# A four-layer network on one core: the start and a norm of the last layer joined with their neighbours, and a 15-tap convolution by even and odd samples

## Time and profile before

| what | value |
|---|---|
| median of three runs | 2219.96 us (2219.67 to 2226.17) |
| the profiled execution, its own time | 2215.92 us |
| its span, first to last instruction | 2214.2 us |
| busy: PE, DVE, ACT, POOL | 83%, 73%, 55%, 30% |
| mean granted TensorE clock | 0.90 of full speed |

### The profile page before, as it was taken

The page is one execution under the profiler, slowest core; times in us unless marked ns, Lnnn a source line. Parts: engine busy times, 40 slices in busy tenths (PEclk is TensorE's granted clock), DMA queues, the critical chain, the costliest instruction groups (busy, mean ns, idle before and its releaser), DMA issues. The chain is left out here.

```text
span 2214.2 us, 45686 instructions
## 1 busy us (share of the span) xinstructions
PE 1846.9 (83%) x17745; PEld 992.8 (45%) x17751; DVE 1612.4 (73%) x2720; ACT 1216.6 (55%) x2472; POOL 674.7 (30%) x755
## 2 busy tenths in 40 slices
PE   2888877866647999999988889999788979887987
PEld 1222221443221335963233357776564434555755
DVE  5999999785779997569963955554756649876367
ACT  2999999532333886258866245556433620221475
POOL 1112120321675542124444633330214620000160
PEclk7899899987876999999989989999789979998986
DMA  8422430100551532733321122212001341430310
GB/s 280 91 58 58 97 77 1 77 19 6 136 190 30 123 59 79 209 76 68 50 32 45 43 65 66 65 53 80 11 23 46 123 142 75 141 94 13 119 53 34
DMA packets 156703, 171.87 MB, mean 78 GB/s; under 512 B 55468, under 2 KB 125174, under 8 KB 156482
## 3 DMA queue, kind: packets, MB, share of 16 engines
q1 hardware_dynamic: 142904, 144.03, 23.8%
q0 software_dynamic: 13584, 24.92, 4.5%
HBM read 95.58 MB, written 77.28 MB: 78 GB/s over the span
## 5 line engine op out<-in xcount | busy, mean ns | idle before, releaser
L464 ACT ACTIVATE a_E<-a_scores,a_nmax 128x512 f32<-128x512 f32 x512 | 343.2, 814 | 14.2 <-DVE a_nmax L397 13.2
L1057 ACT ACTIVATE a_E<-a_scores 128x512 f32<-128x512 f32 x512 | 273.8, 601 | 97.2 <-PE a_scores L1092 92.1
L397 DVE TENSOR_REDUCE a_nmax<-a_scores 128x2 f32<-128x1024 f32 x256 | 302.5, 1217 | 20.8 <-PE a_scores L479 17.1
L961 DVE TENSOR_REDUCE a_nmax<-a_first 128x2 f32<-128x1024 f32 x256 | 295.6, 1217 | 15.2 <-PE a_first L1082 14.0
L479 PE MATMUL a_scores<-a_Vh,a_Kh 48*128 48x512 bf16 x512 | 108.2, 421 | 96.0 <-ACT a_E L464 71.9
L1082 PE MATMUL a_first<-a_Kh,a_Qh 48*128 48x512 bf16 x512 | 148.2, 417 | 36.8 <-PEq L51 20.1
L492 PE MATMUL a_turn<-a_E,a_QS 128*32 128x256 f32 x2048 | 174.1, 417 | 2.3 <-DVE a_QS L407 1.8
L464 ACT ACTIVATION_READ_ACCUMULATOR a_E<-a_scores,a_nmax 128x1 f32 x512 | 167.0, 334 | 0.0
L1092 PE MATMUL a_scores<-a_Qh,a_Kh 51*128 51x512 bf16 x512 | 161.0, 396 | 5.1 <-PEq L51 1.9
L1114 PE MATMUL a_out<-a_E,a_V 128*32 128x256 f32 x2048 | 162.7, 398 | 0.0
L2193 POOL DMA_INDIRECT outs<-f_ye,f_row_at x80 | 78.2, 977 | 144.7 <-ACT f_ye L2314 112.5
(11 more groups left out here) (599 smaller groups left out, 4422.6 us busy)
## 6 DMA issues: line engine op xcount, KB each, us to landing
f_up<-in_L_up SPq DMA_DIRECT2D x32, 256.0 KB, 3.3
a_Kh<-a_rows_k SPq DMA_DIRECT2D x16, 384.0 KB, 6.5
a_Vh<-a_rows_v SPq DMA_DIRECT2D x16, 384.0 KB, 9.9
a_Qh<-a_rows_q SPq DMA_DIRECT2D x32, 192.0 KB, 4.9
a_Kh<-a_rows_k SPq DMA_DIRECT2D x32, 192.0 KB, 5.7
slots<-empty SPq DMA_DIRECT2D x8, 645.0 KB, 6.4
f_xe<-slots SPq DMA_DIRECT2D x40, 129.0 KB, 2.1
outs<-zeros SPq DMA_DIRECT2D x8, 512.0 KB, 4.7
```

Of the source, the lines that this page charges most:

```text
L397: v.tensor_reduce(nmax[:, rd % 2, r1, :, q], bank(b, u)[:], AX.X, ALU.max, negate=True).then_inc(S["max_ready"], 1)
L464: m = a.activation(E[:, u % NE, x], bank(b, u)[:, x], ACT.Exp, bias=nmax[:, rd % 2, r1, x, q:q + 1], accum_out=Z[:, rd % 2, r1, x, q:q + 1])
L961: v.tensor_reduce(out, slot_bank(n)[:], AX.X, ALU.max, negate=True).then_inc(S["slot_read"], 1)
L1057: a.activation(E[:, u % NE, x], ps_s[n % 3][:], ACT.Exp, scale=SCALE).then_inc(S["exp_ready"], 1)
```

## The change

Four edits.

1. **Start.** Blocks one to three become one. x comes in five transfers, the first two of one sequence each; ACT issues the seven weight transfers instead of SP; sequence 0 is normed, turned, projected and split ahead of the others; k is spilled by SP and v by ACT; the first head of each quarter is loaded apart from the others, and the attention's first unit waits for those alone, its ninth for the rest. The parts of sequence 1 are made in block four by POOL. Filling the slots and the small loads move to SP's list in block four, behind the load of each next sequence. ACT splits `parts[2]` instead of POOL, and POOL clears `QS` instead of DVE.
2. **Norm and mix of the last layer.** The three blocks become one: `rows` comes straight from x with a second reciprocal root (variance times (1 + eps), plus eps squared), and turning `rows`, the mix, and turning `XN` go in turns, with one bank each for s, o and the two turned forms.
3. **Inputs of the last attention.** ACT: both sigmoids of q and k, then the gate, then the sigmoid of v. POOL: two row transfers ahead of the gated product instead of one on each side.
4. **Convolution.** For a pair of sequences: y_even from the even taps on even samples (8 products), y_odd from the odd taps on odd samples (7), and one filter of the sums of neighbouring taps on the sums of neighbouring samples (8); each product has 2 x 256 columns. So 92 products instead of 120. POOL adds the taps and the samples and puts the outputs together; ACT copies the banks. The three fetches of expert weights come after all of it, since their room is used for the sums.

```diff
-def attention0(nc, g, w, ahead):
+def load_first_rows(eng, rows, dst, sem, first):
+
+    for x in range(2):
+        src = rows.rearrange("(x q i d) t s -> x (d t) q i s", x=2, q=2, d=HD)[x]
+        heads = dst[64 * x:64 * x + HD * TERMS].rearrange("p (q i) s -> p q i s", q=2)
+        for q in range(2):
+            if first:
+                eng.dma_start(heads[:, q, 0], src[:, q, 0]).then_inc(sem, 16)
+            else:
+                eng.dma_start(heads[:, q, 1:4], src[:, q, 1:4]).then_inc(sem, 16)
...
+                    statistics(0)
+                    variances(0, 0, 1)
+                    roots(0, 0, 1)
+                    normalise(0, R)
...
+                    take_k(v, ps[0][:, 0]).then_inc(S["k_ready"], 1)
+                    v.wait_ge(S["v_made"], 1)
+                    take_v(v, ps[0][:, 1]).then_inc(S["v_ready"], 1)
...
+                    spill_right(a, rows_v[0], parts[:, :, T:2 * T], S["v_spilled"])
+                    query(0)
+                    root(2, EARLY, NB)
+                    a.activation(spare[:], g.ident[:, 0:1], ACT.Exp)
+                    taken(1)
+                    taken(2)
+                    taken(3)
+                    query(1)
+                    for b in range(4, NB):
+                        taken(b)
...
                     load(sp, b, b % 2)
+                    beside(sp, b)
...
-            layer_norm(nc, g, "3", g.X, g.XN, g.XT, ahead=load_weights, again=True)
-            g.recycle_sems()
-            layer_norm(nc, g, "3a", g.XN, rows, HT, scale=ln_cols[:, 0:1], bias=ln_cols[:, 1:2], by_row=True)
...
                     for b in range(NB):
+                        if b + 1 < NB:
+                            turn_rows(b + 1)
                         inputs(b)
+                        turn_x(b)
                         if b:
                             outputs(b - 1)
...
-            conv = [(b, s) for b in range(NB) for s in range(MIXED3)]
-            AHEAD, PER = 78, 3
+            PAIRS = NB // 2
+            SIZES = (EVEN, ODD, EVEN)
+            conv = [(j, n, t) for j in range(PAIRS) for n in range(3) for t in range(SIZES[n])]
+            AHEAD, PER = len(conv) - NHB + 2, 1
...
+                    def add_phases(j):
+                        if j:
+                            pool.wait_ge(S["ms_done"], 3 * j)
+                        x = VT[:, 2 * j:2 * j + 2, PAD3 - 2 * LAG:PAD3 + T].rearrange("c b (k e) -> c b k e", e=2)
+                        pool.tensor_tensor(x_pair, x[:, :, :, 0], x[:, :, :, 1], ALU.add).then_inc(S["x_ready"], 1)
+
+                    def put_together(j):
+                        out = MS[:, 2 * j:2 * j + 2].rearrange("c b (k e) -> c b k e", e=2)
+                        pool.wait_ge(S["ms_read"], 3 * j + 2)
+                        pool.tensor_tensor(out[:, :, :, 0], of_even, of_odd[:, :, 0:HALF], ALU.add)
+                        pool.tensor_tensor(of_even, of_even, of_odd[:, :, 1:1 + HALF], ALU.add)
+                        pool.drain()
+                        pool.wait_ge(S["ms_read"], 3 * j + 3)
+                        pool.tensor_tensor(out[:, :, :, 1], of_both, of_even, ALU.subtract).then_inc(S["ms_ready"], 1)
...
+                        for j, n, t in products:
+                            q = 3 * j + n
+                            if t == 0:
+                                if q >= 2:
+                                    pe.wait_ge(S["ms_read"], q if j + 1 == PAIRS else q - 1)
...
+                            if n < 2:
+                                W, lo = G[:, 2 * t + n], PAD3 + n - 2 * t
+                                x = VT[:, 2 * j:2 * j + 2, lo:lo + T - 1:2]
+                            else:
+                                W = G_pair[:, t] if t < ODD else G[:, 2 * ODD]
+                                x = x_pair[:, :, LAG - t:LAG - t + HALF]
...
-                    convolved(conv[:4 * MIXED3])
+                    BEFORE = 2 * sum(SIZES) + EVEN
+                    a.wait_ge(S["G_ready"], 1)
+                    convolved(conv[:BEFORE])
                     a.wait_ge(S["inverted"], 1)
                     for t in range(NG):
                         a.copy(MT[:, t], M[:, t].rearrange("p c e -> p e c")).then_inc(S["solved"], 1)
-                    convolved(conv[4 * MIXED3:AHEAD])
+                        if t == 0:
+                            convolved(conv[BEFORE:BEFORE + ODD])
+                    convolved(conv[BEFORE + ODD:AHEAD])
                     solved(0)
```

More of the change, by code:

```diff
@@ new lines, in normalise, with remainder @@
+                    def normalise(b, rows):
+                        for r in range(rows):
+                            n, s = divmod(b * R + r, 2)
+                            m = v.tensor_scalar(g.XN[:, b, r], g.X[:, b, r], stats[:, n, s, 1:2], rstd[:, n, s:s + 1],
+                                                ALU.subtract, ALU.mult)
+                        m.then_inc(S["xn_ready"], 1)
+                    def remainder(n, src, part, step, done):
+                        cols = slice(n * T, (n + 1) * T)
+                        v.wait_ge(S[step], n + 1)
+                        v.tensor_tensor(rest[:, cols], src[:, cols], parts[:, part, cols], ALU.subtract).then_inc(S[done], 1)
@@ L313, in _, with root @@
[L313 to L318 removed]
+                    def root(n, lo, hi):
+                        ns = slice(lo * R // 2, hi * R // 2)
+                        a.wait_ge(S["var_ready"], n + 1)
+                        a.activation(std[:, ns], var[:, ns], ACT.Sqrt).then_inc(S["std_ready"], 1)
@@ L3442, in _ @@
                 sigmoid(0, 0)
+                sigmoid(0, 1)
+                gate(0)
                 v_sigmoid(0)
-                sigmoid(0, 1)
-                gate_and_squares(0)
+                squares(0)
                 for b in range(NB):
```

482 lines of the change are left out of this document (307 added, 175 removed).

## The result

The changed kernel has a median of 2211.86 us in 20 runs (2189.87 to 2230.5), the kernel before one of 2223.78 in 20 runs beside it (2214.75 to 2236.91). The ratio is 0.9934, with an interval of 0.9912 to 0.9955: 0.7% or 15 us faster. This ratio goes without five slow runs of the changed kernel, those more than 1.5% above its fastest; the medians of all twenty runs of each are 12 us apart. I had forecast 36 us and a range that ended at 2197. The direction was right, the size was not.

A forecast was written before the change was run, and what follows sets the result against it. It took the start as a chain, PE as the mix's bound, DVE as the loop's, with waits for PE. Terms -19.5 - 9.5 - 1 - 6 = -36 turned 2215.9 into 2180, given as 2181 us; range 2168 to 2197.

The forecast's parts named there:

- Edit 1, -19.5: Start: first scores at 31 us instead of 50.6; bounds -25.5 and -13.
- first product to DVE at 10.8: Start, sequence 0: PE's first projection product reaches DVE at 10.8 us, then k's parts are ready at 15.7.
- Edit 2, -9.5: Norm and mix of the last layer: 47.5 us instead of 57, PE-bound at 4.5 a sequence; bounds -13 and -3.
- Edit 3, -1: Inputs of the last attention: the new order on ACT saves 1 us; bounds -3 and +2.
- Edit 4, -6: Convolution: 12 us gained in the loop, 6 us paid for POOL's adds beside DVE.
- (a): Inversion, late taps and loop: 15 POOL adds slow DVE by 0.4 us each, 6 in all; bounds 0 and 13.
- Gain -12: Loop: fewer products make PE's pass about 3.8 us, under DVE's 5.14, so most of DVE's 15.9 us of waits go.
- The term for `mix_taps`: Loop: after a `mix_taps` PE must wait for DVE and runs late, three places, some 4 us in all.
- The wait (b) of my cost side: Ahead of the loop: the last pair's filter waits for ACT's ninth copy until about 1910, just hidden behind DVE; 4 us above.
- The strided read: Convolution: products on every other sample cost PE nothing extra; the nearest earlier rows showed 12% more for weight loads.
- Rival 1: Convolution gives nothing: waits on DVE's path cost 4 us and POOL's adds 10, total 2189; chance 0.18.
- Rival 5: Start not shortened: first loads wait on full DMA queues or ACT or PE is late, 8 us, total 2189; chance 0.09.

The follow-up runs named there:

- start_own_waits: Changed kernel with the first projection waiting for the k and v weights alone, not all seven weight transfers; first scores at 32.2 us instead of 35.7.
- start_clock: Changed kernel with separate weight waits plus unread products of zeros in PE's idle times of the start; first scores at 30.9 us, ratios 0.9869 and 0.9928 to before.
- small_sums: Changed kernel with POOL's output sums and sample sum cut to 4 columns per pair; inversion 55.6 us instead of 61.5, ratio 0.9899 to before.
- no_conv_warm: Changed kernel with the old convolution and 12 unread products ahead of the router; the router began at the upper clock, which fell at about 478 us.

## Why the prediction was wrong

**What bounds.** The stages were chosen rightly. That DVE owns the time from 1827 to the loop stands: edit 4's cost was paid there, in DVE's time. In the loop PE was late before and is late still, which is where edit 4's gain went.

**Edit 1, -19.5: -15.0.** The step that failed is "first product to DVE at 10.8". It came at 14.5, since PE waited for all seven transfers (12.34), and I had put only their issue into the sum, not the landing of the last beside 2 MB of x. k's parts were ready at 19.8, not 15.7. From there on I had 15.3 to the first scores and it took 15.9. start_own_waits takes the wait away and gets 3.5, start_clock gets the forecast 31. Lesson in the same step: I had taken durations of a PE at its upper clock for a PE that had done nothing yet.

**Edit 2, -9.5: -10.** Right, by its own steps: PE stayed the bound, the period is 4.35 for 4.5.

**Edit 3, -1: 0 to +1.** Within its bounds, and within the scatter. The 24.4 us of ACT's wait for POOL went, and ACT waits 44.4 for PE, up from 15.0: idle time of an engine that was not the bound.

**Edit 4, -6: +5.** Two terms failed, the sign with them. (a) "0.4 us each, 6 in all". The mechanism was the named one, its size 9.8 (6.5 in the inversion, 3.3 in the late taps, which I had at 3.2 and 1.2) before the loop's share, which no run separates. I had priced a POOL add by the *median* of the earlier trace rows, 0.97, and these eight rows mix steps under a POOL add with steps beside none; the worst of them, 1.58, was the one that began just behind a POOL add (1745.60 and 1745.54). An add of 1.2 to 2.1 us costs DVE 0.8. The bound of 13 held. (b) "Gain -12": the loops give 4.8 on average, and DVE's wait for PE fell from 18.5 to 12.8 us on average, not to 4. "PE's pass is about 3.8, under DVE's 5.14" counts busy time. PE's work did shrink as I had it, but with one product a pass PE stands still for 17.2 us of the loop on average instead of 7.1 (the 2.19 us in the middle of a solve is one of these times), and its granted clock is lower. I had written "I take no more off for the clock". Why PE stands still stays open. The term for `mix_taps` was right: three waits of PE, 5.9 us in all against "some 4". The wait (b) of my cost side, "just hides behind DVE", came so: both sides are ready within 0.1 us of each other, and without the adds (small_sums) the wait costs 2.3. The strided read costs 5%, between the nil that I took and the 12% of the earlier trace rows, and changes nothing. The Trainium skill ("SBUF — State Buffer", SBUF: two separate sides) calls such a step free; here it is free to within that 5%. The 1.7 to 2.5 ns an element that the Trainium skill ("Vector Engine (DVE) Microarchitecture Reference", Measured stream behaviour on trn2) has for DVE, where adjacent words take 1.05, does not carry over to PE.

**What was in no term.** -15 - 10 + 0.5 + 5 is -19.5; measured are -15 by the ratio and -12 by the medians. The router with the early start took 9 us more on average than with the old one (42.2 and 33.4), more than the difference; four executions with the old start and ranges of up to 20 us are no proof. I had looked for PE's clock only in the stages that the change touches. The last step of the sum was also wrong: the 4 us between the shown median and the profiled execution make 2184 of 2180, not 2181.

**The rivals.** Rival 1 (the convolution gives nothing, 0.18) had the adds at 10, as they came, and still 2189, since it kept the loop's 12. Rival 5 (the start falls short, 0.09) came by half. Of the 31 us between 2181 and 2211.9, the terms of the edits make 16.5, the router about 9 (not proven), the slip in the last step 3, and the kernel before was itself 4 us slower beside this one than in the runs that I started from. My range allowed for one miss at a time.

## What to carry to other kernels

Price work that is moved onto POOL beside a full DVE by the row that is wholly covered, not by a median: here each add on two tensors in SBUF cost DVE 0.8 us, about the length of one of its own steps. Take PE's duration from a row with the same history: here the products behind its idle times often ran at half speed (2.07 us for 1.16 in the start), and less work in the loop brought more standstill. And before a small difference of medians is believed, run the same kernel twice: a stage that no edit touches can carry 20 us.

## What the hardware showed that I had not expected

PE's granted clock was at its lower level (0.50) for the whole of 52 us in which PE had no idle time, while the same 128 matmul records in the kernel before ran at the upper level from 4 us after their start. In both PE had been idle for 12 us just before (12.3 and 12.5). It also fell in the middle of such a stage (478 us in no_conv_warm). And in the changed kernel's start, seven transfers issued by 4.9 us, of 64 KB and less, landed between 4.6 and 12.3, the last one with 0.5 KB, beside the five transfers of x.
